# Edge list of a graph layer laid out as 128 partitions by 782 columns in place of 125 by 800

## What is computed

```python
hn  = layernorm(x)                                   # 6250 x 256
msg = silu(concat(hn[src], hn[dst], edge_w) @ mW1 + mb1)
msg = silu((layer_norm(msg) * ln_g + ln_b) @ mW2 + mb2)  # per edge
agg = segment_sum(msg, src, 6250)
x   = x + hn + silu(concat(hn, agg) @ uW1 + ub1) @ uW2 + ub2
x   = x + moe(layernorm(x))                          # 8 experts, top 2
```

## Time and profile before

| | |
|---|---|
| time, median of 3 runs | 3877.77 us (3848.03 to 3886.56) |
| profiled execution, its span | 3829.8 us, which is 48.0 us under the median; no other time of that execution is given |
| sorting and node stage | 0 to 907.7 us |
| messages of part 0 | 907.7 to 2243.6 us, 260 pairs |
| messages of part 1 | 2243.6 to 3012.3 us, 182 pairs |
| update, routing, experts, combination | 3012.3 to 3829.8 us |
| busy over the span | PE 62%, PEld 50%, DVE 56%, ACT 42%, POOL 64% |
| POOL's scatters of edge records | 800, 978.8 us in all |
| POOL's gathers | 880 in the trace, 878.0 us in all |

### The profile page before, as it was taken

How to read it: one execution, slowest core, us unless ns; L and a number is a source line. 1 busy time by engine, 2 the same in 40 slices (tenths; PEclk the granted TensorE clock), 3 DMA queues, 4 the chain that set the end, 5 groups by cost and what they waited for, 6 DMA issues and landing times. The chain is left out here.

```text
span 3829.8 us, 64266 instructions
## 1 busy us (share of the span) xinstructions
PE 2378.4 (62%) x13354; PEld 1931.8 (50%) x13355; DVE 2138.5 (56%) x6317; ACT 1598.3 (42%) x5331; POOL 2452.6 (64%) x2433
## 2 busy tenths in 40 slices
PE   0000860002888888888888889999999793059810
PEld 0000540002666666676666668787888673048710
DVE  5997860003565656655565567777777686323222
ACT  0000220002666666666666657777777441023300
POOL 0577777777888888888888856666666353743310
PEclk9999995556999999999999989999999886579965
DMA  3001320001222222222222222222222454333323
GB/s 111 1 2 7 74 63 2 2 2 39 53 52 52 53 53 51 52 52 52 53 53 53 50 61 65 62 65 62 65 63 63 105 156 123 85 96 110 100 96 123
DMA packets 172507, 237.80 MB, mean 62 GB/s; under 512 B 68195, under 2 KB 130509, under 8 KB 171943
## 3 DMA queue, kind: packets, MB, share of 16 engines
q0 software_dynamic: 85728, 144.80, 16.2%
q1 hardware_dynamic: 80352, 86.03, 7.3%
q10 hardware_dynamic: 6375, 6.40, 0.5%
HBM read 172.80 MB, written 63.30 MB: 62 GB/s over the span
## 5 line engine op out<-in xcount | busy, mean ns | idle before, releaser
L258 POOL DMA_INDIRECT edge_records<-stage x800 | 978.8, 1224 | 266.1 <-issue 211.1
L703 POOL DMA_INDIRECT work<-dst_half,stage_i x880 | 878.0, 998 | 247.3 <-issue 229.7
L933 PE MATMUL ps<-W2c,work 128*128 128x256 f32 x3520 | 870.2, 391 | 83.2 <-ACT work L871 59.0
L933 PEld LDWEIGHTS ps<-W2c,work 128*128 128x128 f32 x3520 | 641.7, 192 | 206.1 <-ACT work L871 97.8
L779 DVE TENSOR_TENSOR agg<-agg,ps 125x256 f32 x880 | 366.7, 417 | 552.0 <-remote 355.1
L942 PE MATMUL ps<-work 128*125 128x256 f32 x1760 | 468.4, 389 | 141.1 <-DVE agg L779 141.1
L858 ACT ACTIVATE work<-work 128x512 f32<-128x512 f32 x440 | 277.1, 630 | 496.4 <-DVE work L827 389.0
L942 PEld LDWEIGHTS ps<-work 128*125 128x125 f32 x1760 | 322.6, 189 | 226.2 <-issue 107.9
L852 ACT ACTIVATE work<-ps 128x256 bf16<-128x256 bf16 x440 | 164.2, 373 | 537.5 <-PE ps L903 385.2
L827 DVE SCALAR_TENSOR_TENSOR work<-ps,work,b2c 128x256 f32<-128x256 f32 x880 | 382.3, 476 | 8.5 <-remote 5.2
L913 PE MATMUL ps<-ablk,work 128*128 x2640 | 381.5, 281 | 0.0
(11 more groups left out here) (208 smaller groups left out, 3350.6 us busy)
## 6 DMA issues: line engine op xcount, KB each, us to landing
work<-dst_half,stage_i POOLq DMA_INDIRECT x880
work<-routed_tokens SPq DMA_DIRECT2D x53, 257.0 KB, 2.7
routed_tokens<-work SPq DMA_DIRECT2D x26, 514.0 KB, 7.0
edge_records<-stage POOLq DMA_INDIRECT x800
work<-expert_rows SPq DMA_DIRECT2D x25, 500.0 KB
agg<-in_x SPq DMA_DIRECT2D x5, 1250.0 KB
dst_half<-work SPq DMA_DIRECT2D x50, 125.0 KB
update_node_half<-dpart SPq DMA_DIRECT2D x50, 125.0 KB
```

The source lines that it names most:

```text
L258: pool.indirect_dma_start(recd[h], bass.IndirectOffsetOnAxis(ap=stage[0:NB, i, c, 3:4].bitcast(i32), axis=0), stage[0:NB, i, c, :], None). ...
L703: pool.indirect_dma_start(bg[:, r, u, :], None, dstd, bass.IndirectOffsetOnAxis(ap=stage_i[:, c:c + 1], axis=0)).then_inc(gath[r], 16)
L933: last = t_.matmul(ps[:, 5 + s, u * D:(u + 1) * D], sT[:, a.mod(RT), u, k], W2c[:, k], start=(k == 0), stop=(k == KC - 1))
```

## The change

The edge list is laid out over all 128 partitions. 100,000 is 781 times 128 and 32 more, so there are 782 columns, and the last holds 32 edges; its other 96 places get edges that belong to no block and whose records go to 128 extra rows behind the second record buffer. Part 0 has 462 columns (segments of 66 and 396), part 1 320. A column is 128 records. A staging copy of part 0 takes 33 columns, so part 0 has 14 groups where it had 48. `PAIRS` gives 256 and 185. The loads of edges become three loads of 781 columns and, after a wait for POOL's four small fills of the last column, three loads of 32 edges. The first segment's two groups are written out where there was a loop. Node rows stay on 125 partitions (L290 before, L296 now).

```diff
-ECP = [480, 320]
+EC = -(-E // P)
+EF = E // P
+EL = E - EF * P
+ECP = [462, 320]
-PAIRS = [-(-((n * NB + BK * (P - 1)) // P) // 2) for n in ECP]
+PAIRS = [-(-((n * P + BK * (P - 1)) // P) // 2) for n in ECP]
-TABP = [-(-g // P) for g in GP]
+TABP = [-(-(g + 16) // P) for g in GP]
-SEGS = [[slice(0, 80), slice(80, ECP[0])], [slice(ECP[0], EC)]]
-SC = [10, 5]
+SEGS = [[slice(0, 66), slice(66, ECP[0])], [slice(ECP[0], EC)]]
+SC = [33, 5]
...
-        recE = [rec[0:NB, G0[h]:G0[h] + ECP[h], :] for h in range(2)]
+        recE = [rec[:, G0[h]:G0[h] + ECP[h], :] for h in range(2)]
...
-            nc.gpsimd.tensor_copy(stage[0:NB, i, 0:n], recE[h][:, cols, :]).then_inc(staged, 1)
+            nc.gpsimd.tensor_copy(stage[:, i, 0:n], recE[h][:, cols, :]).then_inc(staged, 1)
...
-                recd[h], bass.IndirectOffsetOnAxis(ap=stage[0:NB, i, c, 3:4].bitcast(i32), axis=0),
-                stage[0:NB, i, c, :], None).then_inc(sems[i], 16)
+                recd[h], bass.IndirectOffsetOnAxis(ap=stage[:, i, c, 3:4].bitcast(i32), axis=0),
+                stage[:, i, c, :], None).then_inc(sems[i], 16)
...
-                sp.dma_start(srci[0:NB], src.rearrange("(p c) -> p c", p=NB)).then_inc(edges_in, 16)
-                sp.dma_start(dsti[0:NB], dst.rearrange("(p c) -> p c", p=NB)).then_inc(edges_in, 16)
-                sp.dma_start(dwt[0:NB], edge_w.rearrange("(p c) o -> p (c o)", p=NB)).then_inc(edges_in, 16)
+                flat = edge_w.rearrange("n o -> (n o)")
+                for full, given in ((srci, src), (dsti, dst), (dwt, flat)):
+                    sp.dma_start(full[:, 0:EF], given[0:EF * P].rearrange("(p c) -> p c", p=P)).then_inc(edges_in, 16)
+                sp.wait_ge(short_set, 4)
+                for full, given in ((srci, src), (dsti, dst), (dwt, flat)):
+                    sp.dma_start(full[0:EL, EF:EC], given[EF * P:E].rearrange("(p c) -> p c", c=1)).then_inc(edges_in, 16)
...
+                nc.gpsimd.memset(srci[:, EF:EC], N).then_inc(short_set, 1)
+                nc.gpsimd.memset(dsti[:, EF:EC], 0).then_inc(short_set, 1)
+                nc.gpsimd.memset(dwt[:, EF:EC], 0.0).then_inc(short_set, 1)
+                nc.gpsimd.iota(pos[:, EF:EC], pattern=[[1, 1]], base=GP[1] * P + P - 1, channel_multiplier=P,
+                               allow_small_or_imprecise_dtypes=True).then_inc(short_set, 1)
...
-                pipeline(pool, groups[0], 0, 2, step)
+                for c in range(groups[0]):
+                    step(Step(0, 2, c))
...
-                e = slice(0, NB)
-                dve.wait_ge(edges_in, 48)
+                e = slice(0, P)
+                dve.wait_ge(edges_in, 96)
```

More of the change, by code:

```diff
@@ L26 @@
 BK = N // NB
-EC = E // NB
-ECP = [480, 320]
+EC = -(-E // P)
+EF = E // P
+EL = E - EF * P
+ECP = [462, 320]
 EC0 = [0, ECP[0]]
-PAIRS = [-(-((n * NB + BK * (P - 1)) // P) // 2) for n in ECP]
+PAIRS = [-(-((n * P + BK * (P - 1)) // P) // 2) for n in ECP]
 GP = [2 * n for n in PAIRS]
@@ L39 @@
 RND = 12582912.0
-assert BK * NB == N and EC * NB == E
+assert BK * NB == N and EC == EF + 1 and 0 < EL < P
 assert sum(ECP) == EC and all(n <= 4 * g for n, g in zip(ECP, GP))
-SEGS = [[slice(0, 80), slice(80, ECP[0])], [slice(ECP[0], EC)]]
-SC = [10, 5]
+SEGS = [[slice(0, 66), slice(66, ECP[0])], [slice(ECP[0], EC)]]
+SC = [33, 5]
 assert all((g.stop - g.start) % (2 * SC[0]) == 0 for g in SEGS[0]) and ECP[1] == 2 * SC[1] * (PAIRS[0] // 8)
@@ L129, in gnn_moe_kernel @@
         ctx.enter_context(nc.allow_non_contiguous_dma(reason="small vectors laid along partitions"))
-        recd = [nc.dram_tensor(f"edge_records{h}", (P * GP[h], 4), f32).ap() for h in range(2)]
+        recd = [nc.dram_tensor(f"edge_records{h}", (P * GP[h] + h * P, 4), f32).ap() for h in range(2)]
         dstd = nc.dram_tensor("dst_half", (N, D), f32).ap()
@@ L143, in gnn_moe_kernel @@
         agg = sb("agg", [P, BK, D])
-        rec = sb("rec", [P, G, 4])
+        rec = sb("rec", [P, G + 8, 4])
         dpart2 = sb("dpart", [P, G * 3], bf16)
@@ L223, in gnn_moe_kernel @@
         edges_in = sem("edges_in")
+        short_set = sem("short_column_set")
         x_in = sem("x_in")
@@ L245, in load_records @@
             sp.dma_start(rec[:, G0[h]:G0[h] + GP[h], :].rearrange("p g f -> p (g f)"),
-                         recd[h].rearrange("(p g) f -> p (g f)", p=P)).then_inc(rec_in, 16)
+                         recd[h][0:P * GP[h], :].rearrange("(p g) f -> p (g f)", p=P)).then_inc(rec_in, 16)
             sp.wait_ge(rec_in, 16 * h + 16)
@@ L303, in _ @@
                 for h in range(2):
-                    sp.dma_start(recd[h].rearrange("(p g) f -> p (g f)", p=P),
+                    sp.dma_start(recd[h][0:P * GP[h], :].rearrange("(p g) f -> p (g f)", p=P),
                                  rec[:, G0[h]:G0[h] + GP[h], :].rearrange("p g f -> p (g f)")).then_inc(pads_out, 16)
@@ L404, in _ @@
                 link(v.tensor_copy(blkh[e], blkf[e]))
-                link(v.memset(pos[e], 0.0))
+                link(v.memset(pos[e, 0:EF], 0.0))
                 link(v.memset(base[e, BK:BK + 1], 0.0))
@@ L482, in _ @@
                                                op0=ALU.mult, op1=ALU.add).then_inc(recs_ready, 1)
+                e = slice(0, NB)
                 dve.wait_ge(x_in, 80)
@@ L576, in _ @@
                     pe.wait_ge(cnt_ready, BK * (h + 1))
-                    nc.tensor.matmul(ps[:, 0, 0:BK], tri[0:NB, :], cnt[0:NB], start=True, stop=True).then_inc(pre_ready, 1)
-                    nc.tensor.matmul(ps[:, 1, 0:BK], onesf[0:NB], cnt[0:NB], start=True, stop=True).then_inc(pre_ready, 1)
+                    nc.tensor.matmul(ps[:, 0, 0:BK], tri, cnt, start=True, stop=True).then_inc(pre_ready, 1)
+                    nc.tensor.matmul(ps[:, 1, 0:BK], onesf, cnt, start=True, stop=True).then_inc(pre_ready, 1)
                 pe.wait_ge(w2g_ready, 2 * KC)
```

## The result

| | before | changed |
|---|---|---|
| median of 4 runs each | 3862.9 us (3841.45 to 3886.56) | 4158.42 us (4151.82 to 4160.51) |
| ratio | 1 | 1.0752 (95%: 1.0695 to 1.0809) |
| profiled span | 3829.8 | 4157.8 |
| first staging copy | 124.7 | 117.2 |
| ranking of part 1 ends | 318.1 | 707.6 |

The forecast was 3621 us. By the profile the sorting stage ends 87.0 us later, part 0 of the messages is 212.4 longer, part 1 27.9, the rest 0.7: together the 328.0 by which the spans differ.

The account below looks back on a forecast made before the run. POOL was taken to bound the sorting stage and part 0's messages, PE part 1's. Terms -169.8 - 7 - 81.0 - 12 + 12.7 = -257.1 us gave a span of 3572.7, plus 48.0, so 3621 us; range 3585 to 3700.

Parts of the forecast that it names:

- Start: Before POOL's first scatter: faster node-row loads and a shorter first DVE segment let POOL begin earlier, -7 us.
- Price of one scatter: Every edge-record scatter on POOL gets 253 ns cheaper with 128 rows; sorting-stage scatters -139.0 us, including 18 fewer columns.
- Gaps, -24.4, and copies, -6.4: Sorting stage, part 0: POOL's time between instructions falls from 174.3 to 149.9 us, staging copies from 12.7 to 6.3.
- Messages of part 0: Message loop: 320 cheaper scatters -81.0 us, four fewer pairs -12; 4.75 us per pair, up to 20 us possibly lost.
- Part 1: Message loop of part 1: 185 pairs for 182, three more at 4.22 us, +12.7 us.
- Nothing after the messages changes: Kernel after 3012.3 us, where part 1's messages end: no change expected.
- On top of the span: Median of runs lay 48.0 us above the profiled span; this was added to the predicted span of 3572.7.
- Is DVE late for POOL?: Sorting stage: DVE's second segment ready near 206 us, node stage over by 575, scattering until 724; no wait for POOL.
- (a): Rival on POOL's scatters: their price does not fall with 128 rows; 3819 to 3842 us, chance 0.08.
- (c): Rival on POOL's scatters: POOL waits for its own DMA queue, so columns cost more; 3991 us, chance 0.03.
- (b): Rival on part 0's messages: PE and waits through ACT and DVE hold 5 us per pair; 3702 us, chance 0.06.
- "Slower": Measured outcome class for the whole kernel: slower than before by over about 1%, some 39 us; chance 0.02.

Follow-up runs that it names:

- chip A: Chip of two edits of the changed kernel: 125 rows per scatter, 3786.95 and 3845.21 us; 11 columns per staging copy, 4138.0; kernel before 3838.6 and 3860.4.

## Why the prediction was right and wrong

**On a chip without the stall** the profiled kernels lie 3782.3 - 3579.6 = 202.7 us apart (two calls, the same chip), where -257.1 was worked out. The mechanism was right there, and its main term was mis-sized: the ratio came to 0.9445 where the forecast had 3621/3878 = 0.934.

- *Start, -7*: right. First ranking 124.4 to 116.9; SP's node rows end 5.9 us sooner.
- *Price of one scatter, -253 ns*: right in kind (rows, not bytes nor direction), mis-sized in place. Until DVE's second segment is over (205 us) 53 scatters took 1342 ns each, as 125-row ones beside a busy DVE had the earlier trace rows; from 310 us on they took 980 ns, the two kinds of rows 8. I had taken the saving off every scatter. The mean came to 1038 in part 0: 479.7 us against 589.3, -110, not -139.0 (the 18 columns fewer are in both).
- *Gaps, -24.4, and copies, -6.4*: 174.3 to 146.6 is -27.7, copies 12.7 to 4.9 -7.8. Right; the groups of 3 give the same price from the other side: 140 more groups cost 855.2 - 755.4 = 99.8 us, 0.71 each, by which the 34 groups that the change saves are 24 us. Messages begin at 755.4, 731 was forecast.
- *Messages of part 0, -93*: -73.3. The scatters fell by 1218 - 999 = 219 ns, 70 us for 320, not 81; the gathers beside them rose from 1015 to 1040 ns, 13 us. PE had 86 in 100 (88 expected), POOL no waits but its own.
- *Part 1, +12.7*: +18.4.
- *Nothing after the messages changes*: +5.0 between these two profiles (813.6 and 818.6), but a second profile of the changed kernel on that chip has 814.4, so it belongs to the spread.
- *On top of the span, 48.0 us*: wrong. The result's profiled execution took 4159.82 for a span of 4157.8, so what lies around a span is 2 us. The 48 were the scatter of that chip's runs, and belonged to no term.

With these the sum is -202.7, and no step of the kernel's own was wrong in sign. Two readings of the rows were loose, and nothing rests on them: PE is busy in two of the first nine slices, not three, and among the slices "at 236 to 410 GB/s" stands one of 149.

**In the result's runs** the failed step is *Is DVE late for POOL?*, by its sentence "The node stage is over by 575 us ... Nothing is late there", and with it the cost of thinner cover in *Messages of part 0* ("up to 20 us of it may be lost"). Both took DVE's pace as given and asked only whether its queue of work was long. Instead, what lies between DVE's instructions grew while POOL scattered at the new pace: the last ranking came 390 us later, and the cover of 150 us (724 - 575) was gone. In part 0 PE's releases come 1.2 to 2.0 us late on average, POOL then waits 287.2 us for DVE, and 6.05 us per pair (1548.3/256) take the place of the forecast's 4.75.

Of the rivals, (a) fell (the price did fall), and (c) named the wrong place: POOL's scatter took 0.96 us, POOL waited for nothing of its own. (b), "a chain of waits through ACT and DVE", was nearest by its place, but its price was a floor of 5 us per pair, with the old pace as its worst; that something could push the chain above the old pace was in no case. "Slower" had a chance of 0.02.

Did a row of before warn? The waits of all engines, 1200 to 2000 us, in the kernel before:

```profile
DVE agg L779 <- remote: 233.2, 68, 4.4
ACT work L858 <- DVE work L827: 140.1, 85, 1.8
PE ps L942 <- DVE agg L779: 89.3, 58, 2.5
ACT work L852 <- remote: 82.1, 56, 2.4
```

And in the kernel before on another chip:

```profile
ACT work L858 <- DVE work L827: 290.7, 149, 3.8
DVE work L827 <- POOL work L711: 218.4, 78, 3.7
```

In a stage bound by POOL, the others' longest wait should lead to POOL. In the trace that I read it led to "remote" instead, 233 us of 800, and I had read the waits of POOL only. PE's releases were late on that chip with 125 rows already: part 1, which has no scatters, took 768.7 us on it and 717.5 on the other, and the kernel 3829.8 and 3782.3. The lateness goes with the scatters, but not with them alone: 0.34 to 0.42 us without any, 1.46 with 125 rows, 1.94 with 128.

**What stays open.** Shown: on chip A scatters of 125 rows leave the old times and scatters of 128 rows (with groups of 11) bring both losses; on four other chips scatters of 128 rows bring neither. Also shown is where the time goes: DVE's sequencer records of 0.70 us in the sorting stage, and PE's late releases in the messages. Not shown: what in the chip makes them. Pace, partitions, and writes as against gathers were never tried in an experiment on a chip that stalls, and the old layout with 128 rows wasn't either, so that the layout has a part in it is not excluded. One observation points somewhere: the traces of the stalling chip hold few landing events of DMAs, 18901 before and 13603 changed, where the other chip's hold 33620 and 33152 for the same work, while the records of DVE's sequencer are complete. The events that release engines and the events that are recorded may share a path that is congested there; that is argued, not shown, and whether the stall exists in an execution that isn't recorded is open too. The Trainium skill, "NOTIFIC — the notification-queue block", section "Overflow: three behaviours, one of which stalls the engine", says that the block which writes such records holds its producers back rather than lose a record inside. The missing records don't fit that sentence well, the late releases would; no run here tells.

## What to carry to other kernels

Price a small indirect DMA by its rows and by what runs beside it: 128 rows of 16 bytes took 0.96 to 1.04 us of POOL where 125 took 1.22, so padding to 128 was worth 4% on the chips without the stall, even with nothing else changed. But before the sum is trusted, read the waits of every engine in the stage, not only of the one that bounds it: where the others wait for "remote" or stand idle on "issue" instead of waiting for the bound engine, look up in the kernel's text which signal they wait for, and compare the end of the instruction that gives it with the start of the one that waits. A gap of microseconds there is something that no duration shows, and a faster producer may bring it out. And measure such a change on more than one chip: the same kernel was 7.5% slower in the runs of the result and some 5.5% faster on two other chips.

## What was not expected of the hardware

- In the result's runs, while POOL sent a scatter of 128 x 16 bytes every 1.26 us, each DVE instruction of the ranking had 2 to 2.7 us of idle time before it, with sequencer records of 0.70 us; elsewhere 5 of 7624 are above 0.3. At one scatter every 1.67 us there was none of it. Operations kept their durations (L493 274 and 275 ns).
- Where the stall was, PE's semaphore updates came 1.2 to 2.0 us after its matmuls' end on average, 0.014 us on the other chips; the updates of DVE, ACT and POOL in the message loop were not late.
- 125 rows cost more of POOL than 128, for scatters of 16 bytes too: 1223 against 1038 ns in the same layout. Beside a busy DVE the advantage is gone: 1376 ns with 128 rows (result) and 1379 with 125 (chip A), from 117 to 203.5 us.
- The message loop without any scatter ran at 4.31 us per pair on the result's chip and 3.98 on the other (796.6 and 735.8 us for 185), at the same granted clock of 1.00, TensorE's 2.4 GHz, in the window from 2600 us; PE had 94.80 and 99.61 in 100 there.
- Each group of 40 scatters in a row had a gap of 2.3 to 2.9 us before its last one, groups of 33 and of 10 had none.
